# A gated cross-attention block: the scratch of y laid out block by block, with two steps moved on SyncE and one on ScalarE

## The reference, cut to what matters

```python
def _L0_xattn_ref(values, keys, query, mask, ...):      # H = 16, D = 16
    v = (values @ Wv + bv).reshape(N, -1, H, D)
    k = (keys @ Wk + bk).reshape(N, -1, H, D)
    q = (query @ Wq + bq).reshape(N, Lq, H, D)
    energy = jnp.einsum('nqhd,nkhd->nhqk', q, k)
    energy = jnp.where(mask == 0, neg, energy)
    attn = jax.nn.softmax(energy / sqrt(D), axis=-1)
    out = jnp.einsum('nhqk,nkhd->nqhd', attn, v).reshape(N, Lq, E)
    return out @ Wo + bo
def _L0_ffn_ref(x, weight, aux_weight1, aux_weight2, bias):
    h = x @ weight @ aux_weight1 @ aux_weight2
    return jnp.tanh(h + bias)
x = x + tanh(g_xattn) * _L0_xattn_ref(ctx, ctx, layernorm(x), mask, ...)
x = x + tanh(g_ffn) * _L0_ffn_ref(layernorm(x), ...)
```

## Time and profile before

| | |
|---|---|
| median of 3 runs | 1084.76 us (1079.82 to 1087.25) |
| profiled execution, its own time | 1090.97 us |
| its span, first to last instruction | 1089.1 us |
| PE busy | 1029.6 us (95%) |
| PEld busy | 895.6 us (82%) |
| DVE busy | 956.2 us (88%) |
| ACT busy | 834.7 us (77%) |
| POOL busy | 803.2 us (74%) |
| granted TensorE clock, mean of the span | 0.989 |
| DMA: bytes, share of 16 engines' time (queue of SP) | 155.72 MB, 51.4% |

### The profile page before, as it was taken

How to read it: one execution, slowest core, us unless ns; L and a number is a source line. 1 busy time by engine, 2 the same in 40 slices (tenths; PEclk the granted TensorE clock), 3 DMA queues, 4 the chain that set the end, 5 groups by cost and what they waited for, 6 DMA issues and landing times.

```text
span 1089.1 us, 45335 instructions
## 1 busy us (share of the span) xinstructions
PE 1029.6 (95%) x18487; PEld 895.6 (82%) x18487; DVE 956.2 (88%) x1331; ACT 834.7 (77%) x1275; POOL 803.2 (74%) x1184
## 2 busy tenths in 40 slices
PE   5888999999999999999999999999999999999964
PEld 5777888888888888888888888888888888888854
DVE  5678989998988999989999999999998999989866
ACT  4466778877877887878888888888878887878842
POOL 5235778878877877877787888788877877877753
PEclk9899999999999999999999999999999999999998
DMA  5134556555555555555656565556555555555442
GB/s 152 44 87 111 136 147 171 142 159 159 147 161 149 164 151 147 171 141 159 162 149 166 152 166 153 165 145 172 149 155 161 145 168 146 160 153 134 133 126 74
DMA packets 260400, 158.87 MB, mean 146 GB/s; under 512 B 174945, under 2 KB 227170, under 8 KB 260194
## 3 DMA queue, kind: packets, MB, share of 16 engines
q1 hardware_dynamic: 260050, 155.72, 51.4%
q10 hardware_dynamic: 144, 0.26, 0.1%
HBM read 85.92 MB, written 68.94 MB: 142 GB/s over the span
## 4 chain that ended last, share of the span: by engine, by line
PE 44%; SPq 16%; DMA 15%; issue 9%; DVE 5%; POOL 5%; ACT 4%; POOLq 0%; ACTq 0%; DVEq 0%
PE ps_m L507 10%; PE ps_m L500 8%; DMA scratch_y<-yn 8%; PE ps_s L636 7%; PE ps_s L615 7%; PE ps_x L647 6%; SPq L215 4%; DMA scratch_m<-max_T 4%; PE ps_m L574 4%; SPq L303 3%; SPq L292 2%; PE ps_s L621 2%; DVE probs L1019 2%; SPq L206 2%; DVE neg_max L1008 1%
## 5 line engine op out<-in xcount | busy, mean ns | idle before, releaser
L1019 DVE TENSOR_TENSOR probs<-ps_s,far_T 128x2048 f32<-128x2048 f32 x128 | 293.0, 2289 | 49.3 <-PE ps_s L636 48.7
L1008 DVE TENSOR_REDUCE neg_max<-ps_s 128x16 f32<-128x2048 f32 x128 | 292.6, 2286 | 28.9 <-PE ps_s L621 28.2
L810 ACT ACTIVATE probs<-probs 128x2048 f32<-128x2048 f32 x128 | 244.6, 1911 | 5.8 <-DVE probs L1019 5.7
L424 POOL TENSOR_TENSOR a_norm<-a_rows,den_wide 128x512 f32<-128x512 f32 x61 | 78.6, 1289 | 119.4 <-issue 116.2
L615 PE MATMUL ps_s<-k_aug,q_aug 32*128 32x128 f32 x4096 | 151.0, 283 | 15.8 <-DVE probs L1019 9.3
L636 PE MATMUL ps_s<-q_aug,k_aug 32*128 32x128 f32 x4096 | 152.3, 284 | 7.8 <-DMA q_aug<-scratch_m 4.6
L615 PEld LDWEIGHTS ps_s<-k_aug,q_aug 32*128 32x128 f32 x4096 | 128.5, 186 | 36.6 <-issue 25.7
L636 PEld LDWEIGHTS ps_s<-q_aug,k_aug 32*128 32x128 f32 x4096 | 127.9, 187 | 26.2 <-DMA q_aug<-scratch_m 7.5
L647 PE MATMUL ps_x<-probs,v_ones 128*32 128x128 f32 x4096 | 140.4, 278 | 4.2 <-issue 3.3
L785 ACT ACTIVATE q_aug<-ps_m,q_bias,q_scale 128x256 f32<-128x256 f32 x256 | 122.8, 559 | 14.9 <-PE ps_s L636 7.9
L647 PEld LDWEIGHTS ps_x<-probs,v_ones 128*32 128x32 f32 x4096 | 105.4, 110 | 33.9 <-issue 33.7
(11 more groups left out here) (123 smaller groups left out, 1779.8 us busy)
## 6 DMA issues: line engine op xcount, KB each, us to landing
scratch_a<-a_den SPq DMA_DIRECT2D x64, 512.0 KB, 3.8
x_in<-in_x SPq DMA_DIRECT2D x64, 256.0 KB, 4.4
a_rows<-scratch_a SPq DMA_DIRECT2D x64, 256.0 KB
den_wide<-scratch_r SPq DMA_DIRECT2D x64, 256.0 KB
out<-y SPq DMA_DIRECT2D x64, 256.0 KB, 4.6
ctx_in<-in_ctx SPq DMA_DIRECT2D x252, 64.0 KB, 2.8
scratch_y<-yn SPq DMA_DIRECT2D x59, 256.0 KB, 4.4
y_blocks<-scratch_y SPq DMA_DIRECT2D x236, 64.0 KB, 2.5
```

The lines of the kernel that those rows point to most:

```text
L424: nc.gpsimd.tensor_tensor(a_norm[:], a_rows[:], den_wide[:], ALU.mult).then_inc(a_norm_ready, 1)
L810: nc.scalar.activation(tile, tile, ACT.Exp).then_inc(probs_ready, 1)
L1008: nc.vector.tensor_reduce(neg_max[:, 0:H].rearrange("p (j c) -> p j c", j=G), ps_s[:], AX.X, ALU.max, negate=True).then_inc(max_ready, 1)
L1019: nc.vector.tensor_tensor(probs[i % 2][:].rearrange("p j s q -> p (j s) q"), ps_s[:].rearrange("p j s q -> p (j s) q"), far_T[:].unsqueeze ...
```

## The change

The scratch of y in DRAM gets the shape [8, 32, 4, 64]: block by block. `write_y` becomes four DMAs of 32 partitions each, in pieces of 256 bytes, where it was one DMA in pieces of 1 KB. `read_y` becomes one DMA in pieces of 1 KB, where it was four in pieces of 256 bytes. The counts of the semaphores follow. On SP `write_max` of the even element now stands ahead of `read_y`, and `read_max` of the odd element stands ahead of `write_y`. On ScalarE `high_of_a` moves from after `keep_v` to between `high_of_x` and `high_of_ctx`, in all turns but the last two, and there it keeps its place.

```diff
-        scratch_y = nc.dram_tensor("scratch_y", [PAIR, P, E], F32, kind="Internal").ap()
+        scratch_y = nc.dram_tensor("scratch_y", [PAIR * G, 32, G, E // G], F32, kind="Internal").ap()
@@ write_y, read_y
                 sp.wait_ge(yn_ready, PAIR * (p + 1))
-                wait(sp, y_blocks_landed, 16 * G * p)
-                sp.dma_start(scratch_y.rearrange("n s e -> s n e"), yn[:]).then_inc(yn_stored, 16)
+                wait(sp, y_blocks_landed, 16 * p)
+                for b in range(G):
+                    sp.dma_start(scratch_y[:, :, b, :].rearrange("na c e -> c na e"),
+                                 yn[b * 32:(b + 1) * 32].rearrange("c n (a e) -> c (n a) e", e=64)).then_inc(yn_stored, 16)
 
             def read_y(p):
-                sp.wait_ge(yn_stored, 16 * (p + 1))
+                sp.wait_ge(yn_stored, 16 * G * (p + 1))
                 wait(sp, y_turned, p)
-                for a in range(G):
-                    sp.dma_start(y_blocks[a * 32:(a + 1) * 32].rearrange("c n (b e) -> c (n b) e", e=64),
-                                 scratch_y[:, :, a * 64:(a + 1) * 64].rearrange("n (b c) e -> c (n b) e", c=32)
-                                 ).then_inc(y_blocks_landed, 16)
+                sp.dma_start(y_blocks[:], scratch_y.rearrange("(n a) c b e -> (a c) n (b e)", n=PAIR)).then_inc(y_blocks_landed, 16)
@@ SP's turn
                 if is_pair(t - 7):
                     store(t - 7)
+                write_max(2 * t)
                 if is_pair(t - 5):
                     read_y(t - 5)
-                write_max(2 * t)
@@
                     read_a(t - 2)
+                read_max(2 * t + 1)
                 if is_pair(t - 4) and t - 4 <= END:
                     write_y(t - 4)
-                read_max(2 * t + 1)
@@ ACT's turn
-                if is_pair(t - 3):
+                if is_pair(t - 3) and not is_pair(t + 2):
                     high_of_a(t - 3)
@@
                     high_of_x(t + 2)
+                    if is_pair(t - 3):
+                        high_of_a(t - 3)
                     high_of_ctx(t + 2)
```

More of the change, by code:

```diff
@@ L402, in normalise_y @@
                 if p <= END + 1:
-                    wait(pool, yn_stored, 16 * p)
+                    wait(pool, yn_stored, 16 * G * p)
                 else:
@@ L987, in turn_y @@
             def turn_y(p):
-                dve.wait_ge(y_blocks_landed, 16 * G * (p + 1))
+                dve.wait_ge(y_blocks_landed, 16 * (p + 1))
                 wait(dve, yT_ready, p)
```

## The result

The changed kernel takes 1105.51 us (median of 6 runs, 1101.77 to 1110.07), the kernel before 1083.07 (6 runs, 1079.82 to 1087.25): the ratio is 1.020, with a 95% interval of 1.0172 to 1.0228. It is slower by 2%, where 1086 was forecast and 1100 was the upper end.

A forecast was written before the change was run, and what follows sets the result against it. Bound: TensorE in most turns, den_wide through a_norm and ScalarE in every third. Sum: 1090.97 - 14.1 + 11.6 + 4 = 1092.5 us, taken 6.2 lower for the timed median: 1086 us, range 1076 to 1100.

The forecast's parts named there:

- ScalarE's step, what it gives: high_of_a after xT: ScalarE no longer stands still for a_norm, so 21 long turns lose up to 14.1 us.
- ScalarE's step, what it costs: GpSimd's rest of a starts 1.15 us later, delaying v_ones; TensorE loses 0.2 us a turn, 11.6 us (5.8 to 17.4).
- SyncE's steps: SyncE queue: maxima go out earlier, counted as nothing; den_wide behind four issues, a_norm 1.0 to 1.4 us later.
- I take 4 us back: Loss over all turns from den_wide going out later, by way of GpSimd: 4 us (ends 0 and 14.1).
- I count nothing: SyncE's reordered maxima: TensorE waited little for either, so no gain or loss was counted.
- The range: 1077 to 1097 us with the ends for the chain of v_ones and for den_wide alone; overall 1076 to 1100.
- The second rival: den_wide bounds by way of GpSimd: issued 1.4 us late, long turns stay as they were; 1098 us, chance 0.20.
- The layout: y's scratch: same bytes and piece counts; the read lands in 3.2 us, in time for VectorE's transpose, costed at nothing.
- The third rival: y's blocks land 0.8 us after VectorE's transpose is due; TensorE loses 0.5 us a turn: 1114 us, chance 0.08.
- The fourth rival: Small writes of y drain at half the rate, den_wide 1.8 us later still: 1130 us, chance 0.04.

The follow-up runs named there:

- experiments 9 and 10: Output bias a turn later: changed kernel, den_wide first, 0.9941; kernel before, high_of_a moved, 0.9957; changed kernel, one write, two half transposes, 0.9887 (0.9923 without late bias).
- experiment 8: Kernel before with only SyncE's order changed (even maxima ahead of the read of y, odd maxima ahead of its write): ratio 1.0153.
- experiment 6: Changed kernel with one write of y in the same 256-byte pieces instead of four (data of y come out mixed): ratio 0.9899.
- experiment 7: Changed kernel without the new layout: one write in 1 KB pieces, four reads in 256-byte pieces: ratio 1.0036 to the kernel before.
- experiment 5: Changed kernel with the four writes of y in 1 KB pieces instead of 256 bytes (data come out mixed): ratio 1.0118.

## Why the prediction was wrong

**ScalarE's step, what it gives: right.** The wait for a_norm is gone, as said. That it returns the long turns held only where a_norm came before GpSimd needed it: in full with one write (no turn over 16.1), hardly in the changed kernel.

**ScalarE's step, what it costs: right in mechanism, half in size.** TensorE's weight loads wait for v_ones 53 times in some 56 turns, and GpSimd waits for the high part of a, 64.5 / 56 = 1.15 us a turn, as worked out. The short turn grew by 0.11, not 0.2: 6 us in place of 11.6. Taking the bias out of the chain gave 15.68 back (experiments 9 and 10), which shows it.

**SyncE's steps: this failed.** "With the price of the four reads, 1.81 us for 0.38, it goes out 1.43 us later" is about right for the median (1.61, of which the order alone makes 0.43), and so is a_norm, forecast 1.0 to 1.4 later and measured 0.96. But I priced four issues by the row of a short turn. 29 of the 59 groups of four took about this, but the other 30 took over 2.2 us, up to 3.61, and den_wide went out up to 3.2 us later. "I take 4 us back" stood in the sum. With the 14.1 gone from a surplus of 15.5 it left some 5 us of long turns; measured are 24.3 over a short turn of 15.79, 23.3 of them in the 27 turns whose a_norm came late. The trace of before had the warning: 46 issues for ctx and 21 for x_in stalled, 56.8 us together, each in a dense row of issues. I read the single write (one stall in 57) and not its neighbours. And "I count nothing" for the order was wrong: experiment 8 has it at 1.5% alone, and 0.7% on top of ScalarE's step.

**The range.** 1077 to 1097 was called the sum with the ends of its two terms, but takes both lower ends for the one bound and only one upper end for the other. With both upper ends it is 1084.8 - 14.1 + 17.4 + 14.1 = 1102, still under the 1105.5 measured.

**The second rival was nearest to what happened.** It named the place (a_norm, y plus th, rstd, xn, the transpose of xn), the threshold of 4.7 us, and 1098; I gave it 0.20. Its price was low, since it left the long turns "as long as they were", when the turns with a_norm past 4.7 us went from 6 to 27. It saw a delay of 1.4 us in every turn and not the stalls; and den_wide did arrive faster than it said, with a_norm 4.43 us after the issue in both turns shown above and 4.82 before.

**The layout.** "In time, and cost it at nothing" holds for the landing (3.2 us, as taken), not for the moment of the issue. VectorE waits for the blocks in 13 turns, 10.8 us in all, and TensorE then waits 4.9 us for the maxima; all 13 are turns that late a_norm makes long anyway. The third rival had this mechanism, but in every turn.

**The fourth rival is out.** 256 KB written by one DMA in 256-byte pieces landed in 3.5 us (experiment 6); in 1 KB pieces from the same place in the queue (experiment 7) it took 3.2, from the old place 4.4. That is nowhere near half the rate, and a kernel that writes so is among the fastest. The Trainium skill (DMA: Bandwidth & Descriptors, Specifications) puts a read-modify-write below 512 bytes. What these runs show of a penalty is small. The SP queue's transfers fill 52.5% of the 16 engines' time in the changed kernel and 50.3% with 1 KB pieces (experiment 5), 577 against 555 us, so by my estimate 0.4 us more of each engine's time for each of the 59 writes; with one write in small pieces (experiment 6) they fill 52.2% of a shorter span, 561 us. The half rate of the rival was my own reading; that section states none.

**Still open:** why an issue stalls. It is seen where many issues follow each other closely, but what holds the issue back at that moment no trace shows. Open, too, are the 11 us by which the medians differ more than the two traces do.

## What to carry to other kernels

Count the issues on a DMA queue, not the bytes or the pieces: putting four issues ahead of an urgent transfer, where one was, costs four issue times and their stalls, and the stalls must be priced from the densest part of that queue, not from the quiet row of a short turn. When a step moves on an in-order engine, list what stands behind it and put the transfer with the least slack (here den_wide) first; that swap alone turned 1.020 into 0.996. And when a wait of one engine is taken away, look which engine will meet the same late transfer next.

## What the runs showed of the hardware

An issue on SyncE's queue took 0.385 us for 1024 pieces of 256 bytes, about as long as each of four for a quarter of them (0.45): here the time of an issue did not grow with its pieces. An issue of a write of y took up to 2.2 us when others stood close ahead of it (of all issues with five others in the 3 us ahead 18% stalled, of those with three or fewer 1.5%); in the 56 turns of the changed kernel the excess of all issues came to 78.9 us. Two VectorE transposes of half the size took 0.64 us each where the whole took 0.68. So halving the elements saved almost nothing here; but the strides on the write side differ as well, and it is one measurement of one shape, not a rule.
